# Expert tiles in two phases: the first sixteen from six of eight groups, taken up when attention ends

## The reference

```python
x = x + tanh(g_xattn[0]) * attention(layernorm(x), ctx, ctx)          # 16 heads of 8
# feed-forward on xf = layernorm(x), T = 4096 tokens
scores = xf @ gate_w + gate_b                                          # 8 experts
topk_vals, topk_idx = top_k(scores, 2)
topk_probs = softmax(topk_vals)
h = relu(einsum('td,edf->etf', xf, w1) + b1[:, None, :])               # 128 -> 512
y = einsum('etf,efd->etd', h, w2) + b2[:, None, :]                     # 512 -> 128
x = x + tanh(g_ffn[0]) * einsum('te,etd->td', combine_w, y)            # two of eight experts a token
```

## Time and profile before

| | us |
|---|---|
| median of 3 runs (lowest, highest) | 519.84 (517.36, 520.61) |
| the profiled execution, device time | 519.43 |
| its span, first to last instruction | 517.6 |
| PE busy | 409.0 (79%) |
| DVE, ACT, POOL busy | 270.9, 274.0, 272.0 (53% each) |

### The profile page before, as it was taken

The page is one execution under the profiler, slowest core; times in us unless marked ns, Lnnn a source line. Parts: engine busy times, 40 slices in busy tenths (PEclk is TensorE's granted clock), DMA queues, the critical chain, the costliest instruction groups (busy, mean ns, idle before and its releaser), DMA issues.

```text
span 517.6 us, 12308 instructions
## 1 busy us (share of the span) xinstructions
PE 409.0 (79%) x4298; PEld 328.9 (64%) x4298; DVE 270.9 (52%) x1003; ACT 274.0 (53%) x816; POOL 272.0 (53%) x297
## 2 busy tenths in 40 slices
PE   0779999999899998999988522099999999999500
PEld 0455666767667576766666411079999999999500
DVE  1355567787776776766757426023333333333187
ACT  0287777878688686877857300034444444444100
POOL 8527138088496794975807256315555555555400
PEclk9979999999999999999989855579999999999855
DMA  3999999400000000000000001628777777777177
GB/s 78 242 370 411 413 364 188 85 12 19 28 13 23 12 12 29 12 28 14 28 6 23 22 11 47 220 67 244 220 246 222 240 222 231 235 227 221 58 241 224
DMA packets 50202, 72.55 MB, mean 140 GB/s; under 512 B 8053, under 2 KB 36733, under 8 KB 50141
## 3 DMA queue, kind: packets, MB, share of 16 engines
q1 hardware_dynamic: 45597, 62.32, 40.3%
q0 software_dynamic: 4544, 9.45, 5.2%
HBM read 41.83 MB, written 34.66 MB: 148 GB/s over the span
## 4 chain that ended last, share of the span: by engine, by line
PE 72%; DVE 9%; issue 7%; POOL 4%; DMA 3%; SPq 2%; ACT 2%; DVEq 0%; POOLq 0%; ACTq 0%
PE S L750 7%; PE T L728 7%; PE U L728 7%; PE O L750 7%; PE S L634 6%; PE O L664 6%; PE O L674 6%; PE T L642 6%; PE S L624 5%; PE U L642 5%; DVE X L1240 4%; DVE PT L1078 2%; POOL zs L962 2%; ACT P L829 2%; PE E L683 2%
## 5 line engine op out<-in xcount | busy, mean ns | idle before, releaser
L829 ACT ACTIVATE P<-S,nmax 128x120 f32<-128x120 f32 x512 | 135.3, 421 | 5.6 <-DVE nmax L1072 5.5
L973 POOL DMA_INDIRECT res<-yo,dpos x78 | 74.9, 960 | 84.3 <-DVE yo L1222 81.3
L962 POOL DMA_INDIRECT zs<-z,posu x64 | 63.4, 991 | 87.8 <-DVE posu L1150 70.2
L1072 DVE TENSOR_REDUCE nmax<-S 128x4 f32<-128x480 f32 x128 | 75.2, 651 | 37.7 <-PE S L634 32.5
L624 PE MATMUL S<-mb_r,I_r 128*128 128x480 f32 x128 | 65.0, 512 | 2.0 <-ACT P L829 1.9
L866 ACT ACTIVATE H<-T,wbuf 128x256 f32<-128x256 f32 x78 | 32.8, 471 | 63.5 <-PE T L728 63.4
L836 ACT COPY PT<-U 120x512 f32<-120x512 f32 x63 | 38.9, 618 | 47.4 <-PE U L642 47.0
L940 POOL TENSOR_SCALAR Kb<-Kt,hm 128x480 f32<-128x480 f32 x32 | 47.0, 1480 | 17.9 <-ACT Kt L850 17.9
L866 ACT ACTIVATE H<-U,wbuf 128x256 f32<-128x256 f32 x78 | 32.7, 471 | 40.1 <-PE U L728 40.1
L930 POOL TENSOR_SCALAR z<-X,mv,rstd 128x128 f32<-128x128 f32 x64 | 50.2, 791 | 3.0 <-POOL rstd L925 2.7
L1084 DVE RECIPROCAL orec<-O 128x128 f32<-128x128 f32 x32 | 30.7, 958 | 37.7 <-PE O L674 37.7
(11 more groups left out here) (150 smaller groups left out, 684.0 us busy)
## 6 DMA issues: line engine op xcount, KB each, us to landing
wbuf<-wpk SPq DMA_DIRECT2D x39, 578.0 KB
zs<-zero SPq DMA_DIRECT2D x1, 17952.0 KB, 60.4
zin<-zs SPq DMA_DIRECT2D x39, 132.0 KB
yg<-res SPq DMA_DIRECT2D x16, 256.0 KB, 3.0
wpk<-in_w SPq DMA_DIRECT2D x1, 2048.0 KB, 58.6
wpk<-in_w SPq DMA_DIRECT2D x8, 256.0 KB, 9.6
out<-X SPq DMA_DIRECT2D x16, 128.0 KB, 2.2
ctx_sb<-in_ctx SPq DMA_DIRECT2D x1, 1440.0 KB, 16.6
```

Of the source, the lines that this page charges most:

```text
L829: ins = nc.scalar.activation(P[:, n % 4, j, :], a[:, j * LK:(j + 1) * LK], ACT.Exp, bias=nmax[:, n % 4, j:j + 1])
L962: nc.gpsimd.indirect_dma_start(out=zs[sb_of(F)], out_offset=bass.IndirectOffsetOnAxis(ap=posu[:, F, k, i:i + 1], axis=0), in_=z2[:, F % 2, ...
L973: nc.gpsimd.indirect_dma_start(out=res, out_offset=bass.IndirectOffsetOnAxis(ap=dpos[:, n % NDP, h:h + 1], axis=0), in_=yo[:, n % NYO, h, ...
L1072: v.tensor_reduce(nmax[:, n % 4, :], Sb[n % NHG][:, 0:HG * LK].rearrange("p (j k) -> p j k", j=HG), AX_X, ALU.max, negate=True).then_inc(m ...
```

## The change

It puts the tiles into two phases: `SB = (6, 2)`. The first takes 16 tiles, all of them full, from the rows of groups 0 to 5 (`FULL`; an expert's tile counts as full in `tot + 1 - TS > j * TS`). The second takes the other 23 slots: what the first phase left of groups 0 to 5, and groups 6 and 7. Both read one buffer `zs` and one count `CU` that goes on over all groups; `used` holds how many tiles of each expert the first phase took. The number of slots in all stays 39. `round_plan` now begins the first phase in round 33 (its `OPENING` in round 32) and hangs 40 of its 68 entries, ten tiles, into rounds 33 to 37. There are two tables, one after group 5's counts (in rounds 29 to 31), one after group 7's (in round 37).

On DVE, part 4 of `route` moves from p = 1 to p = 2 and part 5 from p = 2 to p = 3 (for the last group both stay in round 37). On POOL, the scatters of a group begin at p = 3, one place later than the first of them stood. Group 5, the last of the first phase, is scattered in rounds 30 and 31.

Two changes concern the end: a token's results lie in `res` at `p * 64 + 2 * batch + k` and no longer at `batch * 256 + 2 * p + k`, so that a load of a piece reads 2 KB in one place for each partition (then 1 KB in two places), 32 KB apart from partition to partition; and each output piece is issued five loads behind its own load and no longer after all loads.

```diff
-SCATTERS = {0: (-3, (2, 3)), 1: (-2, (0,)), 2: (-2, ()), 3: (-2, (1,))}
-LAST_SCATTERS = {0: (), 1: (0,), 2: (1, 2), 3: (3,)}
+SCATTERS = {0: (-3, (1, 2)), 1: (-3, (3,)), 2: (-2, ()), 3: (-2, (0,))}
+LAST_SCATTERS = {0: (), 1: (), 2: (0, 1), 3: (2, 3)}
...
-SB = (8,)
+SB = (6, 2)
...
-NTB = [(2 * n * TOK + NE * (TS - 1)) // TS for n in SB]
+FULL = (2 * SB[0] * TOK - NE * (TS - 1)) // TS
+NTB = [FULL, max((2 * NG * TOK + NE * (TS - 1)) // TS - FULL, (2 * SB[1] * TOK + 2 * NE * (TS - 1)) // TS)]
...
-CAP = [n * TOK for n in SB]
-NJ = max(CAP) // TS
-
-ROWS = [NE * c + NE * TS for c in CAP]
+CAP = NG * TOK
+NJ = CAP // TS
+
+ROWS = NE * CAP + NE * TS
...
-NTAB = 10
+NTAB = 13
...
             def load_results(u):
...
-                r0 = TRASH + 2 * LQ * UB * u
-                sp.dma_start(yg[:, u % NYG, :, :, :].rearrange("p i k d -> p i (k d)"),
-                             res[r0:r0 + 2 * LQ * UB].rearrange("(i p k) d -> p i (k d)", p=LQ, k=2)
+                sp.dma_start(yg[:, u % NYG, :, :, :].rearrange("p i k d -> p (i k) d"),
+                             res[TRASH:].rearrange("(p c) d -> p c d", p=LQ)[:, 2 * UB * u:2 * UB * (u + 1), :]
                              ).then_inc(yg_in[u % NYG], 16)
...
             stored(sp, N0[NB])
-            for u in range(u_next, NU):
+            for u in range(NU):
                 load_results(u)
-            for u in range(u_next, NU):
+                if u >= NYG - 1:
+                    result(u - NYG + 1)
+            for u in range(NU - NYG + 1, NU):
                 result(u)
...
-            nc.gpsimd.iota(tok_i[:], pattern=[[2 * LQ, B]], base=TRASH, channel_multiplier=2)
+            nc.gpsimd.iota(tok_i[:], pattern=[[2, B]], base=TRASH, channel_multiplier=2 * B)
...
                     if F + 1 in LAST:
-                        ins = v.tensor_copy(tot[:], bank("RANK", F)[:, GB * NE:(GB + 1) * NE])
+                        ins = v.tensor_scalar(tot[:], bank("RANK", F)[:, GB * NE:(GB + 1) * NE],
+                                              float(1 - TS if F + 1 == LAST[0] else 0), None, ALU.add)
...
-                    then(v.tensor_reduce(nt8[:], tcmp[:], AX_X, ALU.add))
+                    then(v.tensor_reduce(all8[:], tcmp[:], AX_X, ALU.add))
+                    then(v.tensor_tensor(nt8[:], all8[:], used[:, 0:NE], ALU.subtract), False)
+                    then(v.tensor_tensor(g8[:], all8[:], used[:, 1:NE + 1], ALU.subtract))
...
+                    then(v.tensor_tensor(st8[:], end8[:], nt8[:], ALU.subtract))
                     assert count[0] == NTAB
+                    if b == 0:
+                        v.tensor_scalar(left8[:], st8[:], -1.0, float(FULL), ALU.mult, ALU.add).then_inc(used_step, 1)
+                        dve.wait_ge(used_step, 1)
+                        v.scalar_tensor_tensor(used[:, 0:NE], left8[:], 0.0, nt8[:], ALU.max, ALU.min).then_inc(used_step, 1)
...
-                if p < 3 and 0 <= G - 2 < NG:
-                    route(G - 2, {0: 2, 1: 4, 2: 5}[p])
-                if p == 1 and G - 2 == NG - 1:
+                if (p == 0 or p == 1 and G > NG or p == 2) and 0 <= G - 2 < NG:
+                    route(G - 2, 4 if p else 2)
+                if p == 1 and G > NG:
                     route(G - 2, 5)
...
+                if p == 3 and 0 <= G - 2 < NG:
+                    route(G - 2, 5)
                 if p == 3 and 0 <= G - 1 < NG:
                     route(G - 1, 1)
```

More of the change, by code:

```diff
@@ L178, in prior_t @@
     return max([m for m in range(max(n - 3, 0), n) if in_u(m) == in_u(n)], default=-1)
[L181 to L187, removed]
 def sb_of(F):
@@ L243, in sem @@
             return es.enter_context(nc.semaphore(name))
-        zs = [nc.dram_tensor(f"zs{b}", [ROWS[b], ZW], F32, kind="Internal").ap() for b in range(NB)]
+        zs = nc.dram_tensor("zs", [ROWS, ZW], F32, kind="Internal").ap()
         res = nc.dram_tensor("res", [TRASH + 2 * B * LQ, D], F32, kind="Internal").ap()
@@ L336, in build @@
         nt8 = sb("nt8", [128, NE])
+        all8 = sb("all8", [128, NE])
+        g8 = sb("g8", [128, NE])
+        st8 = sb("st8", [128, NE])
+        left8 = sb("left8", [128, NE])
+        used = sb("used", [128, NE + 1])
+        first = sb("first", [128, NB])
         tend = sb("tend", [128, NE, NE])
@@ L372, in build @@
         wpk_done = sem("wpk_done")
-        zs_clear = [sem(f"zs_clear{b}") for b in range(NB)]
+        zs_clear = sem("zs_clear")
         out_done = sem("out_done")
@@ L407, in build @@
         tot_read = sem("tot_read")
+        used_step = sem("used_step")
         scat = [sem(f"scat{r}") for r in range(2)]
@@ L494, in _ @@
             sp.wait_ge(prep_pool, 4)
[L495 to L509, removed]
+            sp.dma_start(zs.rearrange("(p n r) d -> p n (r d)", p=128, r=ZROW // ZW),
+                         zero[:].unsqueeze(1).broadcast_to((128, ROWS // 128 * ZW // ZROW, ZROW))).then_inc(zs_clear, 16)
+            sp.dma_start(wpk[:, :, 0:FF], w1).then_inc(wpk_done, 16)
+            for e in range(NE):
+                sp.dma_start(wpk[e, :, FF:W_B1].rearrange("p (c d) -> p c d", c=NC),
+                             w2[e].rearrange("(c p) d -> p c d", p=128)).then_inc(wpk_done, 16)
+            sp.dma_start(wpk[:, :, W_B1:W_B2].rearrange("e p c -> p e c"),
+                         b1.rearrange("p (e c) -> p e c", e=NE)).then_inc(wpk_done, 16)
+            sp.wait_ge(b2t_done, 1)
+            sp.dma_start(b2d, b2t[:]).then_inc(b2d_done, 16)
+            sp.wait_ge(b2d_done, 16)
+            sp.dma_start(wpk[:, :, W_B2:WROW].rearrange("e p d -> p e d"),
+                         b2d.partition_broadcast(128)).then_inc(wpk_done, 16)
             def load_w(n):
@@ L1160, in table @@
             def table(b, part):
-                NT, BG = NTB[b], SB[b]
-                count = [(0, 3, 7)[part]]
+                NT = NTB[b]
+                count = [(0, 5, 9)[part]]
                 def then(ins, needed=True):
@@ L1329, in _ @@
             made(v.tensor_scalar(tri[:], tri_i[:], 0.0, None, ALU.is_gt), False)
-            for b in range(NB):
-                v.tensor_scalar(ebase[:, b, :], it[:, 0:NE], float(CAP[b]), float(TS), ALU.mult, ALU.add)
+            v.memset(first[:], 1.0)
+            v.memset(used[:], 0.0)
+            v.tensor_scalar(ebase[:], it[:, 0:NE], float(CAP), float(TS), ALU.mult, ALU.add)
             v.tensor_scalar(jt[:], it[:, 0:NJ], float(TS), None, ALU.mult)
@@ L1342, in _ @@
                 round_(k)
-            c = 0
             for b in range(NB):
@@ L1349, in _ @@
                     step([(b, j)])
-                    if b == NB - 1 and j >= COMBINE_FROM:
-                        while c < combined_by(j + 1):
-                            combine(c)
-                            c += 1
-            for n in range(c, 2 * B):
+            for n in range(2 * B):
                 combine(n)
```

58 lines of the change are left out of this document (25 added, 33 removed).

## The result

| kernel | before, us | changed, us | ratio, 95% interval |
|---|---|---|---|
| first comparison | 518.60 (4 runs) | **562.92** (561.34 to 567.48, 4 runs) | 1.0868 [1.0788, 1.0947] |
| the same two kernels later | 509.79 (7 runs) | 480.82 (4 runs) | 0.9425 [0.9374, 0.9475] |
| once more | 508.48 (9 runs) | 481.70 (2 runs) | 0.9478 [0.9407, 0.9549] |

The result to which the prediction of 493 us is held is the first row: 562.92, so the prediction was wrong, and by its sign. The other two rows belong in the same breath. Runs made together form an occasion, and the occasions came in two kinds, told apart by the kernel before alone: on eight it took 508.5 to 511.3 us (kind A), on four 518.6 to 519.5 (kind B). A time and its ratio are always against the kernel before of the same occasion; where times of two occasions are set side by side, they are of one kind.

The account below looks back on a forecast made before the run. PE's work and a 42 us chain between attention and tiles were taken to bound the kernel. 36.8 - 5.0 - 2.5 - 3 = 26.3 us off 519.43 gave 493 us, range 485 to 504.

Parts of the forecast that it names:

- the one on attention: Attention rounds: moved route parts fit into DVE's idle time and scatters a place later cost nothing; 0 us.
- tile stage: From first transposes of tile rows to PE's end: inserted steps, phase change and DVE stalls, -10.5 us together.
- POOL: 0: Rounds 34 to 37: POOL falls 13 us behind PE, stays within yo's six tiles and catches up; 0 us.
- attention rounds longer than before: Sign that would show the 0 us for scatters and route parts moved within attention to be wrong.
- rival E: Stores and loads of res with rows 32 KB apart slow the end; 519 us and more, chance 0.03.
- opening: PE's start on the tiles behind attention moves from 336.8 to 300 us; 36.8 us gained, 34 to 40.
- the end: Combining results: DVE stays the bound with the new layout and output order; 0 us, ends -0.5 and +2.
- small steps: Groups 6 and 7's projection, transposes, gate and counting matmuls now stand between tiles on PE; 5.0 us lost.
- the seam: Between the two phases of tiles: the first runs out, the second opens anew; 2.5 us lost, ends 0.3 and 4.
- VectorE's copies: Rounds 33 to 37: PE waits for copies behind DVE's table and route pieces; 3 us lost, ends 0 and 9.
- rival A: DVE holds PE in rounds 33 to 37; 497 to 506 us with a late opening, chance 0.20.
- D: First phase misses the hole, tiles beginning in round 34 or later; 508 us if they open at 315, chance 0.03.

Follow-up runs that it names:

- held positions: The changed kernel with one GpSimd wait more, so that a round's scatters begin only when its sums are done: 482.03 us against 510.82 (0.9437), kind A.
- rows first: Two phases, old positions, the first two tiles' rows loaded ahead of all weights but the first tile's: 478.07 us against 509.34 before (0.9383), kind A.

## Why the prediction was wrong

**The step that failed** is the one on attention: "Scatters a place later cost nothing there: nothing reads them before the tiles." I asked who reads what they write and who shares their queue, and took for granted that a DMA issue on one engine can't slow another that waits for nothing of it. In kind B it cost 56.4 us of attention. The tile stage lost 28.3 us for 10.5, probably by the same mechanism, which no run tests there. The step "POOL: 0" failed with it: I counted its backlog and asked only whether `yo` could hold it.

**The trace of before had it.** Round 28, PE's timeline, kind B:

```profile
255.14 1.08 PE L664 MATMUL O<-PT,Vm 120*32 120x128 f32 x32
256.04 0.81 PE L674 MATMUL O<-PT,oneV 120*32 120x128 f32 x11
257.15 0.43 PE L674 MATMUL O<-PT,oneV 120*32 120x128 f32 x3 [0.30 <-issue]
...
260.08 1.08 PE L674 MATMUL O<-PT,oneV 120*32 120x128 f32 x12 [0.45 <-issue]
```

while POOL ran four scatters:

```profile
254.36 0.99 POOL L962 DMA_INDIRECT zs<-z,posu  x1 [0.17 <-issue]
...
258.18 0.96 POOL L962 DMA_INDIRECT zs<-z,posu  x1 [0.30 <-issue]
```

6.02 us for a block that takes 1.95 in other rounds. What kept the other rounds nearly free of this was a wait. From the two pages, the scatters of a group before and in the changed kernel, kind B:

```profile
L962 POOL DMA_INDIRECT zs<-z,posu x64 | 63.4, 991 | 87.8 <-DVE posu L1150 70.2
```

```profile
L949 POOL DMA_INDIRECT zs<-z,posu x64 | 63.0, 984 | 20.3 <-issue 17.6
```

Of POOL's 87.8 us idle ahead of its scatters 70.2 were for the positions `posu`. The change moved a group's first two scatters by two rounds (p = 1 to p = 3, not by one place as told above), and by then their positions are there. Without the wait POOL is earlier in each round, and two scatters join the four of p = 0 in one burst. Round 20 shows it: before, the burst of four begins at 192.79, 3.6 us after the block of that round (189.20), and is done when the next has run for 0.9 us; in the changed kernel in kind B the burst of six begins at 213.09 and the block at 213.38. Taking a wait away moved work onto a neighbour that nobody had paired it with. My list of what would be wrong names "attention rounds longer than before", but no rival carried it: rival E's 0.03 for slower sat on the layout of `res`, which cost nothing (combining 23.05 us against 23.16 in the earlier trace rows).

**The other steps held**, in kind A all at once: opening +33.9 for +36.8, since the rows waited for the scatters' landing (they end at 282.96 and the rows are issued at 288.90); tile stage -6.4 for -10.5; the end 0 for 0. In the tile stage PE is busy for 4.4 us more (153.4 against 149.1) where 5.0 of small steps were counted, and idle for 2.1 us more (2.9 against 0.8) where the seam had 2.5 and VectorE's copies 3: its longest wait for VectorE there is 0.9 us, so rival A falls and its 3 us were too many. Sum 27.5 for 26.3, the nearer because 2.9 us of gain too much and 4.1 us of loss too much in the forecast cancel in part, and a ratio of 0.9425 where 493 / 519.43 is 0.949. One sum of chances doesn't close: with "nearly all of D" faster has 0.97 and not 0.94, and E's 0.03 is all that is left for the rest. In kind B the hole went too (42.3 us behind attention's end became 5.5); its gain was real and was paid twice over.

The moved positions brought nothing in kind A: 480.82, 482.31 and 482.03 us with new, old and held positions, and with the wait and rows first the old ones are the better by 5 us (476.95 to 482.02).

**Still open.** What makes an occasion kind A or kind B; no number of the record tells it beforehand, and one chip number stands in both. How a scatter holds PE in kind B: PE idles without a releaser and the sums' semaphore comes 3.5 to 4.7 us after their recorded end in four rounds (from 218.25 to 221.77 in one), 1.1 to 1.3 us behind the end of the burst's last scatter. POOL's ordinary operations beside the block leave it at 1.95 us (the kernel before at 189.20, beside a normalisation). Whether a plain DMA from GpSimd does the same is not known. The moved scatters alone, in one phase, had no run in kind B, and nothing was tried on the bursts of the tile stage.

## What to carry to other kernels

A wait that looks like pure loss may be what keeps two engines' bursts apart: before taking it away, ask what runs beside the freed work, and look in the old trace for one place where the two already met. Hold a burst of indirect DMAs behind the dense block of small matmuls by a semaphore: in kind B one wait made 512.3 into 504.4 us at the old positions, and 562.9 into 506.4 at the new ones (with the load order, whose part is about 1 us there), and it cost nothing clear of noise in kind A (482.0 with it, 480.8 and 481.7 without it on other occasions). Look then whether another operation of that engine lets the burst slip to the next block all the same. And send the kernel before with every comparison: its own level (510 or 519) was what told the two kinds apart, and one occasion alone would have given either +8.7% or -5.8%.

## What the runs showed of the hardware

In kind B indirect scatters issued back to back by GpSimd (0.96 us each, 1.27 apart) go with a slower TensorE beside them. A block of 64 small matmuls at full clock goes from 1.95 to 2.5 or 2.9 us with one (0.73 to 0.96 us of it beside the block), 2.1 to 3.5 with two, 3.9 to 6.0 with three or four, 6.98 with five and 10.05 with seven. Single scatters between tiles cost nothing: in the changed kernel PE is busy for 60.00 us of 60 from 460 to 520 us. After such a stall TensorE's granted clock is at half for about a round, as the row of 348.94 shows (1.96 us for sums that take 1.08 at full clock). In kind A, with the old positions and rows first, 44 scatters in a row from 308 to 364 us left PE 97% busy. The Trainium skill says in SBUF — State Buffer (Who interferes with whom) that DMA never contends with a compute engine. Kind A agrees, with blocks of 1.95 us beside bursts; in kind B a block of 10.05 us does not fit the sentence, and the measurement decides, though no run shows where the two meet.
